# Cross-network kernel on Trainium2: replicated rows and pairs of the next tile moved into PSUM banks, four banks left for pieces

## The reference

```python
e = stack([tbl_f[ids[:, f]] for f in range(39)], axis=1)      # (1024, 39, 16)
x0 = xk = e
for W in (f0, f1, f2):                                        # (39*39,128), (128*39,128), (128*39,128)
    z = einsum('bfd,bgd->bfgd', x0, xk).reshape(b, f * g, d)
    xk = einsum('bpd,pm->bmd', z, W)
    outs.append(xk)
z = sum(concatenate(outs, axis=1), axis=-1)                   # (1024, 384)
h = relu(concatenate([z, dense_ctx], axis=1) @ W_top1 + b_top1)
h = relu(h @ W_top2 + b_top2)
y = h @ W_top3
```

## Time and profile before

| | us |
|---|---|
| median of 3 runs | 1325.23 (1324.9 to 1326.23) |
| the profiled execution, its own time | 1326.9 |
| span of the profiled execution | 1325.1 |
| busy: PE / DVE / ACT / POOL | 1274.4 / 1157.1 / 913.7 / 1052.0 |

### The profile page before, as it was taken

How to read it: one execution, slowest core, us unless ns; L and a number is a source line. 1 busy time by engine, 2 the same in 40 slices (tenths; PEclk the granted TensorE clock), 3 DMA queues, 4 the chain that set the end, 5 groups by cost and what they waited for, 6 DMA issues and landing times. The chain is left out here.

```text
span 1325.1 us, 21626 instructions
## 1 busy us (share of the span) xinstructions
PE 1274.4 (96%) x5983; PEld 1015.7 (77%) x5983; DVE 1157.1 (87%) x3210; ACT 913.7 (69%) x3053; POOL 1052.0 (79%) x743
## 2 busy tenths in 40 slices
PE   3899999999999999999999999999999999999998
PEld 2587777877788777887778877788777877788787
DVE  3599998799988999689996999969998799988983
ACT  2477776677767777577775777757776677767783
POOL 7688888688877888778986888968888688874661
PEclk9799999999999999999999999999999999999999
DMA  5582233332223332213333033331233332223000
GB/s 135 104 206 46 49 62 65 62 62 43 43 52 63 63 65 58 43 34 62 67 64 64 5 64 66 65 61 23 51 62 65 62 58 44 46 54 61 1 3 1
DMA packets 129499, 76.33 MB, mean 58 GB/s; under 512 B 90792, under 2 KB 98201, under 8 KB 129379
## 3 DMA queue, kind: packets, MB, share of 16 engines
q1 hardware_dynamic: 119139, 72.32, 26.8%
q0 software_dynamic: 10240, 2.64, 2.3%
HBM read 68.42 MB, written 3.87 MB: 55 GB/s over the span
## 5 line engine op out<-in xcount | busy, mean ns | idle before, releaser
L397 ACT ACTIVATE parts<-pieces,x_cols 128x128 f32<-128x128 f32 x2560 | 716.0, 376 | 172.3 <-PE pieces L693 156.3
L531 DVE SCALAR_TENSOR_TENSOR parts<-pieces,x_cols,parts 128x128 f32<-128x128 f32 x2432 | 679.9, 341 | 115.5 <-PE pieces L693 89.6
L691 PE MATMUL pieces<-w_hi,cur_hi 128*128 128x512 f32 (+1 forms) x1280 | 548.3, 428 | 18.2 <-DVE parts L531 16.8
L693 PE MATMUL pieces<-w_hi,cur_lo 128*128 128x512 f32 (+1 forms) x1280 | 498.9, 390 | 0.0
L692 PE MATMUL pieces<-w_lo,cur_hi 128*128 128x512 f32 (+1 forms) x1280 | 498.5, 389 | 0.0
L346 POOL TENSOR_TENSOR parts<-parts 128x1024 f32<-128x1024 f32 x127 | 320.1, 2520 | 134.8 <-DVE parts L531 131.4
L337 POOL DMA_INDIRECT emb<-in_table,rows x320 | 345.1, 1078 | 80.9 <-issue 67.4
L691 PEld LDWEIGHTS pieces<-w_hi,cur_hi 128*128 128x128 f32 x1280 | 241.8, 189 | 89.4 <-DVE parts L531 38.4
L693 PEld LDWEIGHTS pieces<-w_hi,cur_lo 128*128 128x128 f32 x1280 | 240.9, 188 | 51.6
L692 PEld LDWEIGHTS pieces<-w_lo,cur_hi 128*128 128x128 f32 x1280 | 242.2, 189 | 47.8
L416 ACT ACTIVATE pairs_hi<-pairs 117x512 fp32r<-117x512 f32 (+1 forms) x224 | 141.9, 634 | 193.8 <-DVE pairs L541 161.9
(11 more groups left out here) (69 smaller groups left out, 594.7 us busy)
## 6 DMA issues: line engine op xcount, KB each, us to landing
partners<-x_wide SPq DMA_DIRECT2D x62, 546.0 KB
partners<-x_wide SPq DMA_DIRECT2D x31, 468.0 KB
x_rep<-x_wide SPq DMA_DIRECT2D x96, 78.0 KB
emb<-in_table,rows POOLq DMA_INDIRECT x320
x_diag<-x_cols SPq DMA_DIRECT2D x256, 10.0 KB
x_wide<-emb SPq DMA_DIRECT2D x32, 80.0 KB
x_wide<-emb SPq DMA_DIRECT2D x32, 32.0 KB
wt<-in_wt SPq DMA_DIRECT2D x1, 1024.0 KB
```

The source lines that it names most:

```text
L397: last = nc.scalar.activation(parts[n % 2][:, 4 * i + r, :], src[:, r * H:(r + 1) * H], ACT.Copy, scale=x_cols[n // 4][:, n % 4, f:f + 1])
L531: nc.vector.scalar_tensor_tensor(acc, src[:, r * H:(r + 1) * H], x_cols[n // 4][:, n % 4, f:f + 1], acc, ALU.mult, ALU.add).then_inc(acc_d ...
L691: nc.tensor.matmul(dst[:, 0:width], hi[:, cols], w1_hi[:, ws], start=True, stop=False)
L693: nc.tensor.matmul(dst[:, 0:width], lo[:, cols], w1_hi[:, ws], start=False, stop=True).then_inc(l2d_ready if q in D_PIECES else l2a_ready, 1)
```

## The change

`x_rep` of the next tile is copied by ScalarE at step 1 into a bank of its own, `x_bank`. `pairs` becomes one bank instead of two SBUF buffers, and the product reads `partners` (SBUF) and `x_bank` and writes `pairs`. The banks for that come from three places: pieces have four instead of five; the turned fields share G's bank (`gx_bank`; 39 rows are turned instead of 78, at s = 17 in every tile); and layer 3 and the top layers use `cur1_bank` between a tile's sum and the next tile's pairs: layer 3 in ten steps of four fields from at = 39, its copy at 49, the first top layer at 79 to 82, its relus at 83 and 84, the second layer at 86 and 87, its relu at 88, the third at 119. The first four Gs of a quad move to at = 49, 53, 60, 64 and the fifth on stay at 10n + 32; `cur2` has three buffers. The first tile's pairs are made in `partners[0]`. New waits keep users of a shared bank apart. Of the diff:

```diff
-XT_ROWS = 2 * F
-X_STEP = XT_ROWS
+X_AT = 320
...
-BANKS = 5
+BANKS = 4
...
-S_G = [2, 12, 22, 32]
-S_G_FIRST = [2, 12, 22, 38]
-L3_STEP = 3
-S_L3 = range(25, 25 + F // L3_STEP)
-S_L3_COPY = 38
-S_H1 = range(41, 41 + N1 // P)
-S_RELU1 = range(45, 47)
-S_H2 = range(50, 50 + N2 // P)
-S_RELU2 = 52
-S_Y = 55
+S_XBANK = 1
+S_X = 17
+G_STEP = {10 * n + 32: (0, n) for n in range(4, BLOCKS - G_LAG)}
+G_STEP.update({49: (0, 0), 53: (0, 1), 60: (0, 2), 64: (0, 3), 2: (1, 13), 12: (1, 14), 22: (1, 15)})
+L3_STEP = 4
+S_L3 = range(39, 39 + (F + L3_STEP - 1) // L3_STEP)
+S_L3_COPY = 49
+S_H1 = range(79, 79 + N1 // P)
+S_RELU1 = range(83, 85)
+S_H2 = range(86, 86 + N2 // P)
+S_RELU2 = 88
+S_Y = 119
+CURS = 3
-S_X = [14, 20, 30, 20]
+def g_made(u, at):
+    late = [s for s, (back, _) in G_STEP.items() if s < at and (back == 0 or u > 0)]
+    return max(0, u * BLOCKS - G_LAG) + len(late)
+def x_turned(u, at):
+    return min(QUADS * TILES, u * TILES + 1 + len([i for i in range(TILES) if 4 * PIECES * i + S_X <= at]))
...
-        pairs = [sb(f"pairs{i}", [KPART, COLS]) for i in range(2)]
-        cur2 = [sb(f"cur2_{i}", [P, H]) for i in range(2)]
+        cur2 = [sb(f"cur2_{i}", [P, H]) for i in range(CURS)]
...
-        xbank = bank("xbank")
+        x_bank = bank("x_bank")
+        pairs = bank("pairs")
         cur1_bank = bank("cur1_bank")
-        gbank = bank("gbank")
-        h_sums = [xbank[:, m * P:(m + 1) * P] for m in range(N1 // P)]
+        gx_bank = bank("gx_bank")
+        x_turns = [gx_bank[:, X_AT + j * F:X_AT + (j + 1) * F] for j in range(4)]
+        h_sums = [cur1_bank[:, m * P:(m + 1) * P] for m in range(N1 // P)]
-        h2_last = [pieces[4][:, m * P:(m + 1) * P] for m in range(N2 // P)]
+        h2_last = [pairs[:, m * P:(m + 1) * P] for m in range(N2 // P)]
...
             def load_partners(tile, i):
+                if tile == 2:
+                    sp.wait_ge(pairs_lo_ready, PAIRK)
...
-                src = xbank[:, 0:4 * X_STEP].rearrange("p (j f) -> p j f", f=X_STEP)
-                nc.scalar.activation(x_cols[i][:, :, 0:F], src[:, :, 0:F], ACT.Copy).then_inc(x_cols_ready, 1)
+                src = gx_bank[:, X_AT:X_AT + 4 * F].rearrange("p (j f) -> p j f", f=F)
+                nc.scalar.activation(x_cols[i][:, :, 0:F], src, ACT.Copy).then_inc(x_cols_ready, 1)
+            def copy_x_rep(tile, i):
+                act.wait_ge(x_rep_loaded[i % 2], (tile - i % 2) * 8 * REP + 16 * REP)
+                act.wait_ge(pairs_ready, tile * PAIRK)
+                nc.scalar.activation(x_bank[0:KPART, :], x_rep[i % 2][:], ACT.Copy).then_inc(x_bank_ready, 1)
             def take_pairs_high(tile, i, k):
-                nc.scalar.activation(pairs_hi[buf][0:rows, :], pairs[buf][0:rows, :], ACT.Copy
-                                     ).then_inc(pairs_hi_ready, 1)
+                src = first_pairs[0:rows, k, :] if tile == 0 else pairs[0:rows, :]
+                nc.scalar.activation(pairs_hi[buf][0:rows, :], src, ACT.Copy).then_inc(pairs_hi_ready, 1)
...
                             weigh_piece(u, n, q)
+                        at = 4 * PIECES * i + s
+                        if more and s == S_XBANK:
+                            copy_x_rep(tile + 1, i + 1)
-                        if more and s == S_X[i] + 1:
+                        if more and s == S_X + 1:
                             copy_x_cols(tile + 1, (i + 1) % TILES)
-                        if s - 1 in (S_G_FIRST if i == 0 else S_G):
-                            if n >= G_LAG:
-                                copy_g(u, n - G_LAG)
-                            elif not first:
-                                copy_g(u - 1, BLOCKS + n - G_LAG)
-                        at = 4 * PIECES * i + s
+                        if at - 1 in G_STEP:
+                            back, b = G_STEP[at - 1]
+                            if u >= back:
+                                copy_g(u - back, b)
...
             def make_pairs(tile, i, k):
-                g, buf, rows = tile * PAIRK + k, (i * PAIRK + k) % 2, rows_of(k)
+                g, rows = tile * PAIRK + k, rows_of(k)
-                    dve.wait_ge(x_rep_loaded[i % 2], (tile - i % 2) * 8 * REP + 16 * REP)
+                    dve.wait_ge(x_bank_ready, tile)
-                wait(dve, pairs_lo_ready, g - 1)
-                nc.vector.tensor_tensor(pairs[buf][0:rows, :], partners[i % 2][0:rows, k, :], x_rep[i % 2][0:rows, :],
+                dve.wait_ge(pairs_lo_ready, g)
+                nc.vector.tensor_tensor(pairs[0:rows, :], partners[i % 2][0:rows, k, :], x_bank[0:rows, :],
...
-                wait(dve, pairs_lo_ready, k - 1)
-                nc.vector.tensor_tensor(pairs[k % 2][0:rows, :], first_banks[k % len(first_banks)][0:rows, :],
-                                        x_rep[0][0:rows, :],
+                nc.vector.tensor_tensor(first_pairs[0:rows, k, :], first_banks[k][0:rows, :], x_rep[0][0:rows, :],
-                nc.vector.tensor_tensor(pairs_lo[buf][0:rows, :], pairs[buf][0:rows, :],
+                src = first_pairs[0:rows, k, :] if tile == 0 else pairs[0:rows, :]
+                nc.vector.tensor_tensor(pairs_lo[buf][0:rows, :], src,
...
             def finish_cur2(u, n):
-                wait(dve, g_ready, g - 1)
+                wait(dve, g_ready, g - CURS + 1)
-                nc.vector.tensor_tensor(cur2[n % 2][:], v[:, 0], v[:, 1], ALU.add).then_inc(cur2_ready, 1)
+                nc.vector.tensor_tensor(cur2[g % CURS][:], v[:, 0], v[:, 1], ALU.add).then_inc(cur2_ready, 1)
...
-            def transpose_x(tile, i, first=True):
+            def transpose_x(tile, i, gs):
-                if i == 2 and not first:
-                    pe.wait_ge(y_copied, (tile - i) // TILES)
+                wait(pe, g_copied, gs)
-                    last = nc.tensor.transpose(xbank[:, j * X_STEP:(j + 1) * X_STEP],
-                                               x_rep[i % 2][0:XT_ROWS, j * P:(j + 1) * P], ident[0:XT_ROWS, 0:XT_ROWS])
+                    last = nc.tensor.transpose(x_turns[j], x_rep[i % 2][0:F, j * P:(j + 1) * P], ident[0:F, 0:F])
-                wait(pe, pairs_ready, k - len(first_banks) + 1)
-                nc.tensor.matmul(first_banks[k % len(first_banks)][0:rows_of(k), :], shift_rows[:, k, 0:rows_of(k)],
+                if first_banks[k] is gx_bank:
+                    pe.wait_ge(x_cols_ready, 1)
+                nc.tensor.matmul(first_banks[k][0:rows_of(k), :], shift_rows[:, k, 0:rows_of(k)],
...
                 if k == 0:
+                    if i == 2:
+                        wait(pe, l3_copied, tile // TILES)
+                    if i == 3:
+                        wait(pe, h2_copied, tile // TILES)
+                    if i == TILES:
+                        wait(pe, y_copied, tile // TILES - 1)
...
-            def make_g(u, n):
+            def make_g(u, n, turned=QUADS * TILES):
+                pe.wait_ge(x_cols_ready, turned)
-                nc.tensor.matmul(gbank[:, 0:FX * BLK_B], cur2[n % 2][:], x_diag[n // 4 % 2][:, n % 4].rearrange("p b f -> p (b f)"),
+                nc.tensor.matmul(gx_bank[:, 0:FX * BLK_B], cur2[g % CURS][:],
+                                 x_diag[n // 4 % 2][:, n % 4].rearrange("p b f -> p (b f)"),
             def layer3(u, step, tiles):
...
```

More of the change, by code:

```diff
@@ L155, in cin_kernel @@
             "p (k r) -> p k r", r=KPART)
-        first_banks = pieces + [gbank]
+        first_banks = pieces + [x_bank, pairs, gx_bank]
+        first_pairs = partners[0]
         x_wide = t["x_wide"]
@@ L178, in cin_kernel @@
         x_cols_ready = sem("x_cols_ready")
+        x_bank_ready = sem("x_bank_ready")
         first_partners = sem("first_partners")
@@ L430, in copy_g @@
                 dst = G[:, n // 4, :, (n % 4) * BLK_B:(n % 4 + 1) * BLK_B]
-                nc.scalar.activation(dst, gbank[:, 0:FX * BLK_B].rearrange("p (b f) -> p f b", f=FX),
+                nc.scalar.activation(dst, gx_bank[:, 0:FX * BLK_B].rearrange("p (b f) -> p f b", f=FX),
                                      ACT.Copy).then_inc(g_copied, 1)
@@ L438, in copy_l3 @@
                 nc.scalar.activation(sum2.rearrange("p (t b) -> p t b", b=TILE_B), G[:, :, F, :], ACT.Copy)
-                nc.scalar.activation(sum3, xbank[:, 0:P], ACT.Copy).then_inc(l3_copied, 1)
+                nc.scalar.activation(sum3, cur1_bank[:, 0:P], ACT.Copy).then_inc(l3_copied, 1)
             def relu1(u, half, sums=h_sums):
@@ L459, in copy_y @@
                 act.wait_ge(y_ready, u + 1)
-                nc.scalar.activation(sum1[0:1, bass.ds(u * P, P)], xbank[0:1, 0:P], ACT.Copy).then_inc(y_copied, 1)
+                nc.scalar.activation(sum1[0:1, bass.ds(u * P, P)], cur1_bank[0:1, 0:P], ACT.Copy).then_inc(y_copied, 1)
             act.wait_ge(w0_summed, 1)
@@ L711, in layer3, with top1_early @@
                     pe.wait_ge(g_copied, (u + 1) * BLOCKS)
-                    pe.wait_ge(x_cols_ready, tiles)
-                for f in range(step * L3_STEP, (step + 1) * L3_STEP):
```

(43 more changed lines are left out.)

## The result

The changed kernel takes 1313.93 us (median of 4 runs, 1313.29 to 1315.42), the kernel before beside it 1325.73: ratio 0.9912, 95% interval 0.9897 to 0.9927. It is faster by 12 us, where 27 were forecast: the time lies inside the range of the prediction, but the gain is less than half of the forecast one. The profiled execution spans 1312.1 us, 13.0 less than before.

What follows compares the result with a forecast made beforehand. TensorE, busy 96% of the span, was taken as the bound, its stalls mostly waits for VectorE. From 1325.1 us, -51 (stalls) + 24 (new waits) - 2 (turned fields) + 2 (first quad) = -27 gave 1298 us, range 1279 to 1318.

Steps and rivals of the forecast that it cites:

- Part 6: Turned fields sharing G's bank, at step 17: no new wait; 39 columns instead of 78 save 0 to 0.12 us each, -2.
- The 51 us to be had: TensorE's stalls, the most that lifting VectorE's holds could win: 45 us in seven quads, 6 in the first quad's tiles.
- part 5: Layer 3 and top in cur1's bank: new TensorE waits; with four banks for pieces, 3.4 us a quad, +24.
- part 3: Four banks for pieces instead of five: VectorE keeps pace, except ahead of piece 37, +0.3 us in one tile of four.
- Part 1: Replicated rows and pairs in PSUM: VectorE's holds go, at most -51 us; operations there cost nothing more.
- (c): Second top layer at step 86: TensorE waits for ScalarE's relus, two pieces ahead instead of four, +1.2 us a quad.
- (d): Pairs at step 90: TensorE waits for ScalarE's relu 2, +1.4 us a quad.
- (a): Layer 3's start at step 39: waits behind cur1's low part and sum on VectorE, +0.3 us a quad.
- (b): Layer 3's copy, from the end of step 48: TensorE gets there before ScalarE's two copies end, +0.2 us a quad.
- The fourth rival: One remaining SBUF operand is still held, so VectorE's holds stay and meet a shorter ring: over 1380 us, chance 0.05.
- The slower rivals: Dearer PSUM operations or too short a ring, 1313 us, chance 0.13; VectorE becoming the bound, 1354 us, chance 0.07.
- the first rival: The new waits for ScalarE hide behind slack, so the 51 us are won whole: 1276 us, chance 0.17.

Runs made afterwards that it cites:

- e2 to e4: The changed kernel with 75, 65 and 64 rows turned in each transpose instead of 39: 1306.52, 1305.14 and 1314.40 us.
- e5: The kernel before, with its pieces in four of its five banks, the fifth unused: 1328.16 us, ratio to before 1.0032.
- e7: The changed kernel with the first top layer, both its relus, the second layer and its relu in earlier steps: 1295.00 us, ratio to before 0.9779.
- e8: The changed kernel with 75 rows turned instead of 39 and the top layers' relus in earlier steps: 1284.95 us, ratio to before 0.9701.
- e1: The kernel before, with 39 rows turned instead of 78, in the old bank and at the old steps: 1327.71 us, ratio to before 1.0008.

## Why the prediction was off

The second quad starts at 191.03 instead of 194.88, -3.9 against a forecast of -4. For the other quads the forecast was 159.5 to 156.3 us; measured were 159.0 to 157.3 in six of them and 150.8 to 151.9 in the last. The span's -13 differs from -27 by 14 us, and two terms of the sum failed:

- **Part 6, the turned fields, failed.** It gave 39 columns "between 0 and half of 0.24 us" and took -2. Measured: +0.25 each, 31 times, +8 us (8.4 between the spans with 39 and 75 rows). The row count was costed as columns only; that it is also the number of rows of the weights was left out, and e2 to e4 show the step between 64 and 65. This is 10 of the 14 us.
- **The 51 us to be had were 44.5.** They were taken from one quad. The fourth takes 159.5, six take 159.0 on average: 6 x 0.5 = 3.0 us too many. The last quad had 2.9 us of stalls, not 6.4: 3.5 too many. A reading of the earlier trace rows was off too: 2.0 of the fourth quad's 6.4 lie in its first two tiles (85.9 against 83.9 for their work), so not nearly all of them in the tiles without layer 3 or top. That the waits of the weight loads summed to 55 was no confirmation (e5).
- **What is left is 3 us the other way.** With 75 rows, so without the first error, a quad still stalls by 156.2 - 153.1 = 3.1 us where part 5 and part 3 made 3.4, the last quad by 151.0 - 147.9 = 3.1, and the first loses 1.3 where + 2 was put down (it ends at 190.0 with 75 rows): 23 us in all where it was 24 + 2. Then 44.5 - 23 - 8.4 = 13. That a quad with 75 rows takes 156.2, as forecast, is therefore partly luck: too much to be had, and waits that are a little too dear.
- **Part 1 held**: products at 686 and low parts at 681 ns on average, nothing more for the output in PSUM. The estimate by the Trainium skill's fixed costs ("VectorE: DVE Perf Modes", TRN2 errata), 0.065 us more each, does not show here: the product's median was 691 with both sources in SBUF and is 685 with one in PSUM.
- **Part 5 held to 0.3 us**: waits of 1.3 (forecast 1.2) and 1.1 (1.4) a quad. With what restarting costs, e7 puts them at 17.6 us in all, 2.5 a quad, where (c) and (d) made 2.6. The rest, (a), (b) and part 3, was forecast at 0.8 a quad, and 153.8 - 153.1 = 0.7 is left in e8. The order of ScalarE's program was enough to work them out.
- **Part 3 held, but the ring's part in the holds did not.** Without holds the ring of four does not throttle, as said. Yet the argument that each hold met a bank with only 2.8 us would have made four banks cost more than the 4 us of e5. The fourth rival's price (+32 for holds with a ring of four) rests on the same step. What sets the loss instead is not shown. One reading is that VectorE's whole work in the busy steps comes near TensorE's, and that the ring only decides where TensorE waits; e1 fits it, where 8 us more for TensorE cost 1 us as long as VectorE was held.
- The slower rivals fell with part 1, and e7 refutes the first rival, in which the new waits hide.

All told: removing the holds and what else the change does was worth about 38 us (e8 against before), of which 18 went to the new waits and 8 to 10 to the rows, and 12 remained.

## What to carry to other kernels

A smaller shape is not always the cheaper one: in this kernel a transpose of 65 rows between full matmuls costs less than one of 64, so it pays to turn rows that nobody uses. Whether small matmuls with more columns do the same was not run. When work moves into a bank with another user, walk the other engine's program from the last input to the first wait: four or five durations gave the new waits to a few tenths of a microsecond, and four constants of the schedule took them back. Take what is to be had from a mean over many periods, not from one, and look at the first and the last by themselves.

## What was not expected of the hardware

- A set of four transposes on 39 or 64 rows between full matmuls costs TensorE 0.25 us more than on 65, 75 or 78 (1.27 with 39 against 1.01 with 75 us around them); a step of 9 us in 1305 from one row.
- VectorE's product of 512 elements with output and one input in PSUM takes 685 ns, the same as from SBUF to SBUF unheld (691).
- ScalarE's copy from SBUF into PSUM (117x512) takes 611 ns, and its high part takes 603 from PSUM where it took 634 from SBUF.
